# The last mixer half of a four-layer kernel in two passes of 256 tokens, and its late tiles' routing steps spaced differently

## The chip, the cores and the metric

The kernel runs on one core of one Trainium2 chip. The metric is the device time of one execution in microseconds (us). Engines are called as the profile calls them: PE is TensorE (PEld its weight loads), DVE is VectorE, ACT is ScalarE, POOL is GpSimd and SP the engine that issues most transfers.

## What is computed

2,048 tokens of 512 numbers pass through four residual layers, each behind a layer norm. The change touches the third layer and the routing of the fourth.

```python
x = x + scan_layer(norm(x))      # state space scan, 16 states
x = x + ffn_layer(norm(x))       # Hadamard transforms, gate / up / down
# third layer ("mixer"); y = conv(W_in_x . x) * D, z = silu(W_in_z . x)
x = x + einsum('bsi,hi->bsh', y * z, W_out)
# fourth layer: 64 experts, 8 per token, at most 128 tokens per expert
w, sel = top_k(softmax(x @ gate_w.T), 8)
pos = running_count_of_each_expert_over_tokens   # in token order
slot = where(pos < 128, pos, dropped)
out = down_e(silu(gate_e(inp)) * up_e(inp))      # per expert
x = x + weighted_sum_of_the_token's_experts
```

## The kernel before

Tokens are held in 4 chunks of 512, each of 4 tiles of 128 tokens, so there are 16 tiles. The ffn and mixer layers are cut into "halves" (list `HALVES`), and each half into **quanta**: for every 128 inner channels (a "pair") one gate quantum and one up quantum, and after them one down quantum per pair. A gate or up quantum is 12 products with 512 moving tokens (4 blocks of 128 inputs, times 3, since each operand is split into a high and a low part). Its weights are 512 KB, which come through a ring of 6 buffers: SP loads the buffer for quantum q + 6 as soon as quantum q has been used (`load_ring`).

Every engine runs a program that is written out by hand in **positions**. `spread` gives each position its quanta. At position p PE does the quantum of p, ACT and DVE work on the results of p - 1 and p - 2 (tanh, `half_gated`, `gated`, `gated_hi`, `gated_lo`), and everything else that an engine does in p stands behind that. In the stretch of this change every position has one quantum. The last mixer half (chunk 3, 8 pairs) starts at position TURN + 12; its down products are done after the loop by `tail(t, js)`, tile by tile.

**Routing** of a tile i has six steps, each in its own position, counted from `route_at[i]`. The steps, with their lines in the trace of before:

- `finished` (DVE, L1154 and L1407: mean and variance) and `rstd` (POOL, L1607 and L1609: reciprocal root, two instructions).
- `route(i, 0)` (DVE, L1368: the normalised tile `row`; it waits for `rstd(i)`).
- `route_T` (PE L568, then ACT L1080: transposes; they wait for `row`).
- `logits` (PE L784) and `route(i, 1)` (DVE, from L1372 to L1385, with `route_exp` on ACT).
- `place` (PE L790 and L791) and `route(i, 2)` (DVE, L1389 to L1396; the last writes `idx`).
- `rows_out` (POOL, L1600): eight indirect scatters of the tile's rows into the experts' slots, the first of which waits for `idx`.

Steps stand one position apart. Tiles 8 to 11 (chunk 2) start at TURN + 12 and every 4 positions after it; tiles 12 to 15 wait for the down products of the last half and are written out behind the loop. The position counter takes POOL through `rows_out(i)` in four positions with two scatters each, and `rstd` of a later tile stands where its position comes. SP starts the expert stage when all scatters have landed (L550, loads of `xe`).

Of the kernel before, what the change touches and what calls it, by code (L numbers as in the profile page):

```python
# [14 lines left out]
CH = 512  # L15
NCH = T // CH
# [22 lines left out]
MIX = [[("mixer", c, part, 4 * part, 4) for part in range(2)] for c in range(NCH - 1)] + [[("mixer", NCH - 1, 0, 0, M1)]]  # L39
# [12 lines left out]
H4 = hadamard(4).astype(int)  # L52


def build(nc, a):
# [47 lines left out]
    with top:  # L103
# [20 lines left out]
        with A:  # L124
# [176 lines left out]
            route_at = [DRAIN + 12 + 5 * i for i in range(EARLY)] + [TURN + 12 + 4 * i for i in range(TT)]  # L301
# [19 lines left out]
            def used(q):  # L321

                h, kind, j = quanta[q]
                if kind == "gate":
                    return S_g, first_pair[h] + j + 1
                if kind == "up":
                    return S_up, first_pair[h] + j + 1
                if j < pairs_of[h] - 1:
                    return S_dk, first_pair[h] - h + j + 1
                return S_dm, TT * (h + 1)  # L330
# [6 lines left out]
            def before_half(h):  # L337
# [4 lines left out]
                return half_of[kind, c, part - 1] if part else half_of["ffn", c, 1]  # L342

            with nc.Block() as block:
# [17 lines left out]
                def _(sp):  # L362
# [138 lines left out]
                    for pos in range(LAST):  # L501
# [23 lines left out]
                        if pos == TAIL + TT + 3:  # L525
                            sp.wait_ge(S_de, TT * len(HALVES))
# [12 lines left out]
                        if pos == TAIL - 6:  # L539
# [12 lines left out]
                    sp.wait_ge(S_dm, TT * len(HALVES))  # L552
# [11 lines left out]
                def _(pe):  # L564
# [11 lines left out]
                    def quantum(h, kind, j):  # L576
# [3 lines left out]
                        if kind != "down":  # L580
                            w = w.rearrange("p (k s c) -> p k s c", k=KT, s=2)
                            x = tokT[c % 2]
                            b = PF[2 * (j % 2) + (0 if kind == "gate" else 1)]
                            if kind == "gate":
# [12 lines left out]
                            for k in range(KT):  # L597
                                nc.tensor.matmul(b[:, :], w[:, k, 0, :], x[:, 0, k, :], start=(k == 0), stop=False)  # L598
                                nc.tensor.matmul(b[:, :], w[:, k, 0, :], x[:, 1, k, :], start=False, stop=False)  # L599
                                last = nc.tensor.matmul(b[:, :], w[:, k, 1, :], x[:, 0, k, :], start=False, stop=(k == KT - 1))  # L600
# [4 lines left out]
                        for t in range(TT):  # L605
# [12 lines left out]
                    def tail(t, js):  # L618
# [3 lines left out]
                        for j in js:  # L622
# [6 lines left out]
                            if (t, j) == (0, 0):  # L629
                                pe.wait_ge(S_de, TT * h)  # L630
# [166 lines left out]
                    for pos in range(DRAIN, TAIL):  # L797
# [10 lines left out]
                        for i, base in enumerate(route_at):  # L808
                            if pos == base + 4:
                                place(i)  # L810
                        for i, base in enumerate(route_at):
                            if pos == base + 3:
                                logits(i)
                        for i, base in enumerate(route_at):
                            if pos == base + 2:
                                route_T(i)
                        side(pos)
                    first_part, second_part = range(M1 // 2), range(M1 // 2, M1)
                    place(11)
                    tail(0, range(M1))  # L820
                    tail(1, first_part)
                    route_T(12)
                    tail(1, second_part)
                    logits(12)
                    tail(2, first_part)
                    place(12)
                    route_T(13)
                    tail(2, second_part)
                    logits(13)
                    tail(3, first_part)  # L830
                    place(13)
# [4 lines left out]
                    place(14)  # L836
# [871 lines left out]
```

## Time and profile before

| What | us |
|---|---|
| median of 3 runs | 1709.13 |
| lowest and highest of them | 1702.77, 1710.74 |
| the profiled execution | 1722.31 |
| its span, first to last instruction | 1720.5 |
| of the span: until the last mixer half starts | 1226 |
| from there to the last scatter | 119 |
| expert stage and sums after it | 375 |

The profiled execution is 1.8 us longer than its own span, and 13 us longer than the median. Instants below are microseconds from the start of the span.

### The profile page before, as it was taken

The page shows a single profiled execution, that of the slowest core. Times are in us where ns is not written, and L with a number is a line of the kernel's source. Part 1 is how long each engine was busy: PE and PEld are TensorE (multiplying, and loading weights), DVE is VectorE, ACT ScalarE, POOL GpSimd, SP SyncE. Part 2 cuts the span into 40 slices and gives each one's busy share as a digit, 9 for nine tenths or more (in the row PEclk, how much of TensorE's full clock was granted, in tenths as well). Part 3 has the DMA queues.
Part 4 walks back from the last instruction along what each step waited for, and adds up shares of the span by engine and source line. Part 5 has one row for each costly group of instructions (what it writes and reads, how often), then busy time and mean ns, then how long its engine had stood idle before and what let it go on. Part 6 is the DMA issues. An engine that isn't in the chain of part 4 may idle for free. (4 is left out here: it accounts for less than half of the span.)

```text
span 1720.5 us, 18848 instructions
## 1 busy us (share of the span) xinstructions
PE 1505.0 (87%) x5792; PEld 1038.6 (60%) x5792; DVE 1049.3 (61%) x1535; ACT 587.0 (34%) x1050; POOL 784.6 (46%) x483
## 2 busy tenths in 40 slices
PE   6989966899857999888999989999985699999990
PEld 2444323577645777776787878888874355555550
DVE  4887679798789887889888865452454122222220
ACT  4444633343534244534333332121321133233220
POOL 3467854253744345634445434773257322222232
PEclk8999987999978999999999999999997799999995
DMA  6899764256663666667565557998761599999997
GB/s 205 247 281 266 213 199 163 73 157 190 202 180 126 187 205 213 188 202 268 154 186 186 173 166 248 369 370 256 241 211 54 174 327 324 321 317 311 305 252 135
DMA packets 193539, 380.39 MB, mean 221 GB/s; under 512 B 20994, under 2 KB 95106, under 8 KB 192944
## 3 DMA queue, kind: packets, MB, share of 16 engines
q1 hardware_dynamic: 165360, 322.89, 59.7%
q0 software_dynamic: 20032, 39.92, 9.8%
q10 hardware_dynamic: 8064, 16.55, 2.8%
q8 instruction: 42, 0.69, 0.2%
q14 instruction: 41, 0.34, 0.1%
HBM read 301.65 MB, written 124.35 MB: 248 GB/s over the span
## 5 line engine op out<-in xcount | busy, mean ns | idle before, releaser
L1518 POOL TENSOR_TENSOR y<-y,hc 128x2048 f32<-128x2048 f32 x64 | 293.1, 4579 | 255.5 <-DVE hc L1350 255.5
L598 PE MATMUL bank<-tokT,ring 128*128 128x512 f32 x768 | 309.1, 402 | 13.9 <-DVE xall L1202 7.2
L1332 DVE TENSOR_TENSOR_SCAN bx<-bank,state,bx 128x512 f32<-128x512 f32 x256 | 312.7, 1267 | 0.8
L600 PE MATMUL bank<-tokT,ring 128*128 128x512 f32 x768 | 303.7, 395 | 0.0
L599 PE MATMUL bank<-tokT,ring 128*128 128x512 f32 x768 | 303.4, 395 | 0.0
L975 ACT ACTIVATE bank<-dl,an 128x512 f32<-128x512 f32 x256 | 171.0, 684 | 330.6 <-DVE bx L1332 330.5
L1524 POOL TENSOR_TENSOR act<-th,act 128x512 fp32r<-128x512 f32 x88 | 116.0, 1318 | 260.3 <-ACT act L899 259.7
L854 PE MATMUL bank<-wgu,xeT 128*128 128x384 f32 x512 | 178.5, 492 | 5.9 <-DMA wde<-wd_in 4.5
L598 PEld LDWEIGHTS bank<-tokT,ring 128*128 128x128 f32 x768 | 146.8, 191 | 50.6 <-issue 17.6
L600 PEld LDWEIGHTS bank<-tokT,ring 128*128 128x128 f32 x768 | 146.7, 191 | 32.4
L610 PE MATMUL bank<-ring,act 128*128 128x512 f32 x352 | 143.7, 408 | 24.7 <-DVE th L1182 19.4
L599 PEld LDWEIGHTS bank<-tokT,ring 128*128 128x128 f32 x768 | 146.8, 191 | 29.8
L1350 DVE TENSOR_TENSOR hc<-bx,bank 128x2048 f32<-128x2048 f32 x64 | 146.0, 2282 | 26.2 <-PE bank L686 25.6
L1323 DVE TENSOR_TENSOR bx<-u,bank 128x2048 f32<-128x2048 f32 x64 | 146.0, 2281 | 11.9 <-PE bank L678 8.8
L1600 POOL DMA_INDIRECT slots<-row,idx x128 | 127.0, 992 | 53.9 <-issue 41.4
L612 PE MATMUL bank<-ring,act 128*128 128x512 f32 x352 | 140.6, 399 | 0.0
L611 PE MATMUL bank<-ring,act 128*128 128x512 f32 x352 | 140.5, 399 | 0.0
L1175 DVE SCALAR_TENSOR_TENSOR th<-th,bank 128x512 f32<-128x512 f32 x96 | 65.7, 684 | 111.9 <-ACT th L894 96.7
L854 PEld LDWEIGHTS bank<-wgu,xeT 128*128 128x128 f32 x512 | 93.1, 192 | 60.4 <-issue 6.7
L1652 POOL DMA_INDIRECT acc<-ye,tok x32 | 49.3, 1541 | 163.6 <-DMA acc<-ye,tok 129.6
L871 PE MATMUL bank<-wde,hT 96*128 96x512 f32 x256 | 120.6, 593 | 0.5 <-DVE hT L1500 0.5
L1490 DVE SCALAR_TENSOR_TENSOR te<-te,bank 128x192 f32<-128x192 f32 x64 | 22.7, 354 | 154.0 <-ACT te L1123 154.0
(151 smaller groups left out, 2106.3 us busy)
## 6 DMA issues: line engine op xcount, KB each, us to landing
ring<-w_all SPq DMA_DIRECT2D x286, 512.0 KB
wgu<-wgu_in SPq DMA_DIRECT2D x64, 768.0 KB
wde<-wd_in SPq DMA_DIRECT2D x64, 384.0 KB
slots<-empty_in SPq DMA_DIRECT2D x16, 1154.0 KB, 8.8
w_all<-staged_u SPq DMA_DIRECT2D x64, 256.0 KB, 3.1
xe<-slots ACTq DMA_DIRECT2D x56, 288.5 KB
w_all<-fst SPq DMA_DIRECT2D x48, 256.0 KB, 3.8
w_all<-staged_d SPq DMA_DIRECT2D x32, 256.0 KB, 3.8
```

The lines of the kernel that those rows point to most:

```text
L598: nc.tensor.matmul(b[:, :], w[:, k, 0, :], x[:, 0, k, :], start=(k == 0), stop=False)
L599: nc.tensor.matmul(b[:, :], w[:, k, 0, :], x[:, 1, k, :], start=False, stop=False)
L600: last = nc.tensor.matmul(b[:, :], w[:, k, 1, :], x[:, 0, k, :], start=False, stop=(k == KT - 1))
L610: nc.tensor.matmul(PF[t][:, :], act8[:, 0, j, tok], w[:, 0, :], start=(j == 0), stop=False)
L611: nc.tensor.matmul(PF[t][:, :], act8[:, 0, j, tok], w[:, 1, :], start=False, stop=False)
L612: last = nc.tensor.matmul(PF[t][:, :], act8[:, 1, j, tok], w[:, 0, :], start=False, stop=(j == pairs - 1))
L854: last = nc.tensor.matmul(CG[i % 2][:, 0:2 * FE], xeT[:, i % 2, k, :], wgu[i][:, k, :], start=(k == 0), stop=(k == KT - 1))
L975: nc.scalar.activation(dA[k % 2][:, :], dl[c % 2][:, k, :], ACT.Exp, scale=an[:, k, n:n + 1]).then_inc(S_dA, 1)
L1323: nc.vector.tensor_tensor(bx[:, :, :], u[:, :, :], PB[:, :].unsqueeze(1).to_broadcast([P, KT, CH]), ALU.mult).then_inc(S_bm, 1)
L1332: nc.vector.tensor_tensor_scan(bx[:, k, :], dA[k % 2][:, :], bx[:, k, :], state[:, k, n:n + 1], ALU.mult, ALU.add).then_inc(S_sc, 1)
L1350: nc.vector.tensor_tensor(hc[:, :, :], bx[:, :, :], PC[:, :].unsqueeze(1).to_broadcast([P, KT, CH]), ALU.mult).then_inc(S_cm, 1)
L1518: nc.gpsimd.tensor_tensor(y[c % 2][:, :, :], y[c % 2][:, :, :], hc[:, :, :], ALU.add).then_inc(S_ya, 1)
```

## The change

The last mixer half becomes two (`LASTS`): the first takes tiles 12 and 13 (256 of the 512 tokens) through gate, up and down, the second tiles 14 and 15. Both use the same 8 pairs, so the weights of the gate and up quanta are loaded twice, and so are those of the down quanta but for the two that are held. Each gate or up quantum has 12 products of 256 moving tokens, each down quantum of the first pass 6 products (two tiles). Only the down products of tiles 14 and 15 are left to `tail`. The second pass swaps the PSUM banks (`pair_banks`), and its first gate waits for `gated` of the last pair before it.

Tiles 8 to 11 start every 6 positions in place of 4, tiles 12 and 13 get places in the loop (HALF1 and HALF1 + 4), and the steps of these six tiles stand 0, 1, 4, 6, 8 and 9 positions behind the tile's start in place of 0 to 5. Three loads of expert weights move to other positions of SP.

```diff
-MIX = [...] + [[("mixer", NCH - 1, 0, 0, M1)]]
+MIX = [...] + [[("mixer", NCH - 1, part, 0, M1) for part in range(2)]]
+LASTS = (len(HALVES) - 2, len(HALVES) - 1)
+def columns(h):
+    return slice(CH // 2 * LASTS.index(h), CH // 2 * LASTS.index(h) + CH // 2) if h in LASTS else slice(0, CH)
+def tiles_of(h):
+    return range(2 * LASTS.index(h), 2 * LASTS.index(h) + 2) if h in LASTS else range(TT)
+def pair_banks(h, j):
+    first = 2 * ((j + (h == LASTS[1])) % 2)
+    return first, first + 1
...
-            TAIL = TURN + 12 + 2 * M1
+            HALF1 = TURN + 12 + 3 * M1
+            TAIL = HALF1 + 2 * M1
-            spread([("mixer", 2, 1), ("mixer", 3, 0)], range(TURN, TAIL + RING))
+            spread([("mixer", 2, 1), ("mixer", 3, 0), ("mixer", 3, 1)], range(TURN, TAIL + RING))
-            route_at = [DRAIN + 12 + 5 * i for i in range(EARLY)] + [TURN + 12 + 4 * i for i in range(TT)]
+            route_at = [DRAIN + 12 + 5 * i for i in range(EARLY)] + [TURN + 12 + 6 * i for i in range(TT)] + [HALF1, HALF1 + 4]
+            ROUTE_EARLY, ROUTE_LATE = (0, 1, 2, 3, 4, 5), (0, 1, 4, 6, 8, 9)
+            route_step = [[base + d for d in (ROUTE_EARLY if i < EARLY else ROUTE_LATE)] for i, base in enumerate(route_at)]
...
-                        if pos == TAIL - 6:
+                        if pos == TURN + 26:
                             ...
                             load_weights(5, 5)
-                        if pos == TAIL - 1:
+                        if pos == HALF1 + 2:
                             ...
                             load_weights(6, 6)
-                        if pos == TAIL + 2:
+                        if pos == TAIL:
+                            sp.wait_ge(S_up, sum(pairs_of))
                             load_weights(7, 7)
...
                                 if j >= 2:
                                     pe.wait_ge(S_hg, i - 1)
+                                elif h == LASTS[1]:
+                                    pe.wait_ge(*((S_gt, i) if j == 0 else (S_de, adds_to(h) + 2)))
...
-                                nc.tensor.matmul(b[:, :], w[:, k, 0, :], x[:, 0, k, :], start=(k == 0), stop=False)
+                                nc.tensor.matmul(b[:, cols], w[:, k, 0, :], x[:, 0, k, cols], start=(k == 0), stop=False)
...
-                        for t in range(TT):
+                        for t in tiles_of(h):
...
-                    tail(0, range(M1))
-                    tail(1, first_part)
...
+                    tail(2, range(M1))
+                    tail(3, range(0, 3))
                     route_T(14)
-                    tail(3, second_part)
+                    tail(3, range(3, 5))
                     logits(14)
+                    tail(3, range(5, 7))
+                    place(14)
+                    tail(3, range(7, M1))
                     route_T(15)
...
-                            if pos == base + 4:
+                            if pos == at[4]:
                                 route(i, 2)
...
-                            if pos == base + 1:
+                            if pos == at[1]:
                                 route(i, 0)
```

The rows below are the engines' programs as built; a name with a number is a buffer, `bank4` to `bank7` hold the quanta's products, `n4_*` the statistics of routing.

On DVE, in the loop, the work that ends with `idx` of tile 9 and the work on `row` of tile 10, before:

```order
L1396 TENSOR_SCALAR idx<-top8 128x8 [waits route_step]
L1397 TENSOR_TENSOR chosen_sum<-chosen_sum,chosen_b 128x64
L1398 TENSOR_SCALAR number<-number 128x1
L1154 BN_STATS n4_st6<-xall 128x6 [waits down_added]
L1407 BN_AGGR n4_mvt<-n4_st6 128x2 [waits n4_bn]
L1175 SCALAR_TENSOR_TENSOR th<-th,bank4 128x512 [waits tanh_done]
L1191 TENSOR_TENSOR act8<-th,act8 128x512 [waits gated_hi,gated]
L1368 TENSOR_SCALAR row<-xall,n4_mvt,n4_rst 128x512 [waits n4_rs,rows_out2]
```

The same place in the changed program:

```order
L1174 BN_STATS n4_st6<-xall 128x6 [waits down_added]
L1430 BN_AGGR n4_mvt<-n4_st6 128x2 [waits n4_bn]
L1196 SCALAR_TENSOR_TENSOR th<-th,bank4 128x256 [waits tanh_done]
L1214 TENSOR_TENSOR act8<-th,act8 128x256 [waits gated_hi,gated]
L1391 TENSOR_SCALAR row<-xall,n4_mvt,n4_rst 128x512 [waits n4_rs,rows_out2]
L1204 SCALAR_TENSOR_TENSOR th<-bank5,cs,th 128x256 [waits half_gated,up_mm]
L1412 TENSOR_TENSOR rt<-bank3,rt 128x64 [waits place_mm]
L1413 TENSOR_SCALAR rt<-bank3 128x64
L1415 TENSOR_TENSOR rt<-rt 128x64 [waits route_step]
L1417 MAX top8<-rt 128x8 [waits route_step]
L1419 TENSOR_SCALAR idx<-top8 128x8 [waits route_step]
```

Before, `idx` of tile 9 was written ahead of the statistics of tile 10 and of its `row`. Now the statistics and `row` of tile 10 stand ahead of `idx` of tile 9.

On POOL, the last scatters (DMA `slots`) and `rstd` pairs (L1607, L1609) of before, from the last five scatters of tile 11 to the end of those of tile 13:

```order
L1600 DMA slots<-row,idx 8192x577 x5
L1607 TENSOR_TENSOR n4_vet<-n4_mvt,eps 128x1 [waits n4_mv,constants_ready]
L1609 TENSOR_TENSOR n4_rst<-n4_vet,neghalf 128x1 [waits n4_ve]
L1600 DMA slots<-row,idx 8192x577 [waits route_step]
L1600 DMA slots<-row,idx 8192x577
L1607 TENSOR_TENSOR n4_vet<-n4_mvt,eps 128x1 [waits n4_mv,constants_ready]
L1609 TENSOR_TENSOR n4_rst<-n4_vet,neghalf 128x1 [waits n4_ve]
L1600 DMA slots<-row,idx 8192x577 x6
L1607 TENSOR_TENSOR n4_vet<-n4_mvt,eps 128x1 [waits n4_mv,constants_ready]
L1609 TENSOR_TENSOR n4_rst<-n4_vet,neghalf 128x1 [waits n4_ve]
L1600 DMA slots<-row,idx 8192x577 [waits route_step]
L1600 DMA slots<-row,idx 8192x577 x7
```

And of the change, from the last seven scatters of tile 12 to the end of those of tile 15:

```order
L1614 DMA slots<-row,idx 8192x577 x7
L1614 DMA slots<-row,idx 8192x577 [waits route_step]
L1614 DMA slots<-row,idx 8192x577 x7
L1621 TENSOR_TENSOR n4_vet<-n4_mvt,eps 128x1 [waits n4_mv,constants_ready]
L1623 TENSOR_TENSOR n4_rst<-n4_vet,neghalf 128x1 [waits n4_ve]
L1614 DMA slots<-row,idx 8192x577 [waits route_step]
L1614 DMA slots<-row,idx 8192x577 x2
L1621 TENSOR_TENSOR n4_vet<-n4_mvt,eps 128x1 [waits n4_mv,constants_ready]
L1623 TENSOR_TENSOR n4_rst<-n4_vet,neghalf 128x1 [waits n4_ve]
L1614 DMA slots<-row,idx 8192x577 x5
L1614 DMA slots<-row,idx 8192x577 [waits route_step]
L1614 DMA slots<-row,idx 8192x577 x7
```

Before, the `rstd` of tiles 14 and 15 stood ahead of most of the scatters of tiles 12 and 13. Now the `rstd` of tile 14 stands behind all the scatters of tiles 12 and 13. In both programs the loop has each `rstd(i + 2)` behind all eight scatters of tile i, for i of 8 to 10.

## Rows read from the trace of the kernel before

**Rows 1.** Busy time by stage; the header names the columns, (x) counts instructions.

```profile
core 0: us, PE busy (x) PEld busy (x) DVE busy (x) ACT busy (x) POOL busy (x), PEclk, DMA share, GB/s
1226.00:1311.00 85.00, 78.65 (x382) 63.37 (x381) 43.88 (x154) 17.63 (x41) 42.97 (x52) 0.98 0.60 195
1311.00:1346.00 35.00, 4.07 (x22) 3.39 (x21) 7.27 (x38) 1.78 (x7) 26.42 (x29) 0.54 0.11 31
1346.00:1720.50 374.50, 323.46 (x1152) 186.62 (x1152) 81.88 (x320) 96.55 (x192) 102.07 (x68) 0.94 0.99 283
```

**Rows 2.** The chain that ended last, where the expert stage begins: start us, us, what.

```profile
1346.51 2.95 DMA xe<-slots
1349.50 1.97 PE bank L845 x8
```

**Rows 3.** Costliest group of the stretch 1226 to 1346.

```profile
L1600 POOL DMA_INDIRECT slots<-row,idx x64 | 63.2, 988 | 25.6 <-issue 23.1 <-DVE idx L1396 2.6
```

**Rows 4.** GpSimd in order of time: start us, us, instruction [idle before <-releaser].

```profile
1242.71 1.04 POOL L1600 DMA_INDIRECT slots<-row,idx  x1 [0.19 <-issue]
...
1257.55 1.04 POOL L1600 DMA_INDIRECT slots<-row,idx  x1 [0.19 <-issue]
...
1266.55 0.97 POOL L1600 DMA_INDIRECT slots<-row,idx  x1 [0.31 <-issue]
...
1291.23 0.23 POOL L1607 TENSOR_TENSOR n_vet<-n_mvt,eps 128x1 f32<-128x1 f32 x1
1291.54 0.57 POOL L1609 TENSOR_TENSOR n_rst<-n_vet,neghalf 128x1 f32<-128x1 f32 x1
...
1301.93 1.04 POOL L1600 DMA_INDIRECT slots<-row,idx  x1 [2.57 <-DVE idx L1396]
...
1306.40 1.04 POOL L1600 DMA_INDIRECT slots<-row,idx  x1 [0.19 <-issue]
...
1344.34 0.97 POOL L1600 DMA_INDIRECT slots<-row,idx  x1 [0.30 <-issue]
```

**Rows 5.** VectorE in order of time, same columns.

```profile
1240.41 0.17 DVE L1396 TENSOR_SCALAR idx<-top 128x8 uint32<-128x8 f32 x1
...
1269.65 0.21 DVE L1389 TENSOR_TENSOR rt<-bank,rt 128x64 f32<-128x64 f32 x1
...
1270.55 0.17 DVE L1396 TENSOR_SCALAR idx<-top 128x8 uint32<-128x8 f32 x1
...
1292.21 0.55 DVE L1368 TENSOR_SCALAR row<-xall,n_mvt,n_rst 128x512 f32<-128x512 f32 x1 [1.48 <-POOL n_rst L1609]
...
1300.95 0.17 DVE L1396 TENSOR_SCALAR idx<-top 128x8 uint32<-128x8 f32 x1
...
1314.80 0.55 DVE L1368 TENSOR_SCALAR row<-xall,n_mvt,n_rst 128x512 f32<-128x512 f32 x1 [0.80 <-POOL n_rst L1609]
...
1321.89 0.42 DVE L1396 TENSOR_SCALAR idx<-top 128x8 uint32<-128x8 f32 x1
```

**Rows 6.** The page's groups of instructions: two widths of one VectorE operation.

```profile
L1175 DVE SCALAR_TENSOR_TENSOR th<-th,bank 128x512 f32<-128x512 f32 x96 | 65.7, 684 | 111.9 <-ACT th L894 96.7
...
L1490 DVE SCALAR_TENSOR_TENSOR te<-te,bank 128x192 f32<-128x192 f32 x64 | 22.7, 354 | 154.0 <-ACT te L1123 154.0
```

**Rows 7.** TensorE in order of time.

```profile
1261.38 1.00 PE L784 MATMUL bank<-gate,x4T 128*128 128x64 f32 x8
1262.18 0.48 PE L598 MATMUL bank<-tokT,ring 128*128 128x512 f32 x1
...
1267.94 0.39 PE L598 MATMUL bank<-tokT,ring 128*128 128x512 f32 x1
...
1270.43 0.39 PE L600 MATMUL bank<-tokT,ring 128*128 128x512 f32 x1
```

**Rows 8.** A window in which transfers fill the DMA engines, columns as in the first group.

```profile
1241.00:1248.00 7.00, 7.00 (x36) 5.64 (x35) 3.03 (x6) 1.98 (x4) 4.81 (x7) 1.00 1.03 351
```

**Rows 9.** DMA issues between 1226 and 1346.

```profile
ring<-w_all SPq DMA_DIRECT2D x17, 512.0 KB
```

More of the change, by code:

```diff
@@ L38 @@
 FFN = [[("ffn", c, part, HALF * part, HALF) for part in range(2)] for c in range(NCH)]
-MIX = [[("mixer", c, part, 4 * part, 4) for part in range(2)] for c in range(NCH - 1)] + [[("mixer", NCH - 1, 0, 0, M1)]]
+MIX = [[("mixer", c, part, 4 * part, 4) for part in range(2)] for c in range(NCH - 1)] + [[("mixer", NCH - 1, part, 0, M1) for part in range(2)]]
 HALVES = FFN[0] + [h for c in range(2, NCH + 1) for h in MIX[c - 2][:1] + FFN[c - 1] + MIX[c - 2][1:]] + MIX[NCH - 1]
@@ L341, in before_half @@
                     return None
-                return half_of[kind, c, part - 1] if part else half_of["ffn", c, 1]
+                return half_of[kind, c, part - 1] if part and h not in LASTS else half_of["ffn", c, 1]
             with nc.Block() as block:
@@ L582, in quantum @@
                             x = tokT[c % 2]
-                            b = PF[2 * (j % 2) + (0 if kind == "gate" else 1)]
+                            cols = columns(h)
+                            b = PF[pair_banks(h, j)[0 if kind == "gate" else 1]]
                             if kind == "gate":
@@ L807, in _ @@
                                 mixer_T(c, t)
[L808 to L809 removed]
+                        for i, at in enumerate(route_step):
+                            if pos == at[4]:
                                 place(i)
[L811 to L812 removed]
+                        for i, at in enumerate(route_step):
+                            if pos == at[3]:
                                 logits(i)
[L814 to L815 removed]
+                        for i, at in enumerate(route_step):
+                            if pos == at[2]:
                                 route_T(i)
                         side(pos)
[L818 to L831 removed]
+                    tail(2, range(M1))
+                    tail(3, range(0, 3))
                     route_T(14)
[L833 removed]
+                    tail(3, range(3, 5))
                     logits(14)
+                    tail(3, range(5, 7))
+                    place(14)
+                    tail(3, range(7, M1))
                     route_T(15)
[L836 removed]
                     logits(15)
@@ L893, in tanh @@
                         wait(act, S_al, i - 1)
-                        nc.scalar.activation(th[:, i % 2, :], PF[2 * (j % 2)][:, :], ACT.Tanh, scale=gsh[:, m:m + 1]).then_inc(S_th, 1)
+                        cols = columns(h)
+                        nc.scalar.activation(th[:, i % 2, cols], PF[pair_banks(h, j)[0]][:, cols], ACT.Tanh, scale=gsh[:, m:m + 1]).then_inc(S_th, 1)
                     def gated_hi(h, j):
@@ L898, in gated_hi @@
                         i = first_pair[h] + j
-                        nc.scalar.activation(act8[:, 0, j, :], th[:, i % 2, :], ACT.Copy).then_inc(S_ah, 1)
+                        cols = columns(h)
+                        nc.scalar.activation(act8[:, 0, j, cols], th[:, i % 2, cols], ACT.Copy).then_inc(S_ah, 1)
                     def prep_hi(i, m):
@@ L1108, in _ @@
                     side(TAIL + 1)
-                    for i in range(3 * TT, NCH * TT):
+                    for i in range(len(route_at), NCH * TT):
                         route_T(i)
@@ L1528, in side @@
                         for h, kind, j in quanta_at.get(pos - 2, ()):
-                            if kind == "up" and h < len(HALVES) - 1:
+                            if kind == "up" and h not in LASTS:
                                 gated_lo(h, j)
```

102 lines of the change are left out of this document (46 added, 56 removed).

## Prediction

> **What bounds the kernel now.** I read the stages first. From 1226, where the last mixer half starts, PE is busy for 78.7 of 85 us, but from 1311 to 1346 for only 4.1 of 35, while POOL is busy for 26.4 of those 35 and DMA is idle at a share of 0.11 [rows 1]. The chain of waits enters the expert stage through the `xe` loads at 1346.51 and PE follows at 1349.50 [rows 2]; the loads wait for the last scatter. So the stretch ends with POOL, not with PE. There are 64 scatters in it, of 988 ns each [rows 3]; eight of them take 9.97 us from the first one's start (1257.55) to the last one's end (1267.52) [rows 4], so one is 1.28 us with its gap. From 1306.40 to the end at 1345.31 POOL does nothing but scatter, apart from one `rstd` [rows 4]. Whatever PE gains is worth something only if POOL's last scatter ends sooner. The expert stage behind it (374.5 us [rows 1]) is untouched.
>
> POOL has 64 times 1.28 = 82 us of scatters and started at 1242.71 [rows 4], so 21 of the 103 us until 1345.31 are waits and `rstd`. That is what the change can win or lose.
>
> **PE and DMA with 256 tokens.** Twelve 512-token products from the start of 1267.94 to that of 1270.43 are 11 steps, 226 ns each [rows 7], so a quantum is 2.72 us. 512 columns at 2.4 GHz are 213 ns, so 13 are fixed. For 256 columns no row exists. From below, half of 226: 113. From above, a weight load that could not hide: eight loads with 64 columns each pass in 0.80 us (1261.38 to 1262.18 [rows 7]), 100 ns per pair, and 107 ns of streaming behind it gives 207. I take 107 + 13 = 120 ns, since the 100 ns row shows that loads can come at that rate: a quantum is 1.45 us. All quanta of the half then cost 32 x 1.45 + 8 x 1.36 (first pass down) + 24 x 2 x 0.226 (tail) = 68.1 us against 16 x 2.72 + 96 x 0.226 = 65.2 before: 3 us more on PE.
>
> By the Trainium skill, TensorE: Matmul & The Clock Gate, section Back-to-back issue gap, a warm product takes N/2.4 + 2.5 ns. At 512 columns this case's row has 226 where the rule has 216; at 256 the rule would give 109 ns in place of 120 and start the first scatter about 1 us sooner.
>
> Ring loads: 46 quanta have weights of 512 KB [rows 9], 40 of them loaded after the half starts, 21 MB. The x store, the two held blocks and three experts' weights that fall into the stretch add about 5.6 MB by the sizes in the program. When full, DMA moves 351 GB/s (share 1.03) [rows 8]: 76 us. PE needs 68 plus eight tiles of routing at 1.3 (0.4 transposes, 0.8 logits [rows 7], 0.1 place), 78 us. So DMA is nearly as full as PE; ring waits of up to 4 us are likely near the held and expert loads, but PE has slack against POOL, as follows.
>
> **The order of POOL and DVE.** This is the term that decides. Scatters of tile i, then `rstd(i + 2)` is POOL's order before and now. Before, `idx(i + 1)` stood on DVE ahead of `row(i + 2)`; now it stands behind it, and `row(i + 2)` waits for `rstd(i + 2)`. So tile i + 1 cannot start scattering until all eight scatters of tile i are done, then `rstd`, `row`, a `gated`, the five instructions of `route(i + 1, 2)`, and the wake of POOL. One turn:
>
> - eight scatters, 9.97 [rows 4];
> - `rstd`, 0.88 (1291.23 to 1292.11) [rows 4];
> - to the start of `row` 0.10, `row` 0.55 [rows 5];
> - `gated` on 256 columns: 684 ns at 512 columns, 354 at 192 [rows 6], so 0.42 on that line; the second operation is a little slower, and I take 0.48, which stands in two of the three turns (a down position has none);
> - `route(., 2)` from 1269.65 to 1270.72, 1.07 [rows 5];
> - `idx` written (1301.12 [rows 5]) to scatter (1301.93 [rows 4]), 0.81;
> - less 0.2 for neighbouring records on DVE that overlap.
>
> That is 13.7 (13.2 without `gated`), of which POOL idles 2.8. PE's own pace over six positions is 6 x 1.45 + 1.3 = 10.0 us, so POOL and DVE set the pace and PE waits 3 to 4 us per tile. ACT and DVE queues behind `row` (tanh results, `gated`) are late with it, and PE's `route_T` of that tile too, but all of that waits for the same `rstd`. These waits also hide the ring's.
>
> The Trainium skill says, in TensorE: Matmul & The Clock Gate, section Architectural detail: the array is 16× 32×32, not 1× 128×128, that ScalarE, VectorE and GpSimd run their queues strictly first in, first out; only weight loads overtake. The trace agrees: DVE's `row` at 1292.21 waited for `n_rst` and everything on DVE with it [rows 5].
>
> **The sum.** `idx(8)` ended at 1240.58 [rows 5]. Now eight short quanta stand ahead of it in place of four long ones (11.6 for 10.9, +0.7), and `finished(9)` and `row(9)` are now ahead of it on DVE (+0.8): 1242.1. POOL wakes 0.81 later: scatters of tile 8 at 1242.9 (before 1242.71, since `rstd(9)` was in the way).
>
> - Tiles 9, 10, 11 start at 1256.6, 1269.8, 1283.5 (turns of 13.7, 13.2, 13.7).
> - Tile 11's scatters have `rstd(13)` in their middle (+0.8), so they end at 1294.3; `idx(12)` comes about then, four more position's work on DVE after `row(13)`: tile 12 at 1295.
> - Tile 12 and 13 run on, 10.2 each: done at 1315.2. PE's tail for tile 14 ends near 1309 and waits.
> - `rstd(14)` 1316.1, `row(14)` 1316.2. Tile 15's chain from `row` to `idx` took 7.5 before (1314.80 to 1322.31 [rows 5]), at the low clock (0.54 granted [rows 1]). Tile 14's now has 12 products of tile 15 between its steps, 2.7 us at 0.226, of which most hide behind ACT and DVE steps: 8.3. `idx(14)` 1324.5, three scatters from 1325.3 to 1328.9.
> - `rstd(15)`, `row(15)` at 1329.9; `idx(15)` 7.5 later, 1337.4; the five remaining scatters of tile 14 are done by 1336.3. Wake 0.81, eight scatters 9.97: **1348.2**.
>
> Before, 1345.31 [rows 4]: +2.9 us. The profiled 1722.3 would become 1725.2; on the median of the runs, 1709.1 + 2.9 = **1712**. The x store of the last chunk leaves at about 1327 and takes some 5 us, still under the scatters. The moved expert loads are wanted from 1350 on and are covered.
>
> **Rivals.**
>
> - *The order costs nothing and POOL packs.* Were each `idx` ready when POOL is, 1242.9 + 82 + six `rstd` of 0.8 = 1330, a gain of 15 us: 1694. For it speaks that tiles 12 and 13 are routed in the loop, and that PE is ahead of POOL. Against it is the built order of DVE. If only the loop's three idles (2.8, 2.3, 2.8) vanished, the end would be 1340, 1704, which is within 0.5%. It ends under 1700.6 if 8.5 us of POOL's 19 idle go. Chance 0.13.
> - *Weight loads set the pace of 256 columns.* At 190 ns per product (the upper half of the bounds) a quantum is 2.3 us and six positions with routing 15 us, more than the turn of 13.7. `idx(8)` is 5.5 us later, the two turns whose six positions are gate and up quanta are 1.3 longer, and two more positions' groups for tile 12: about +9 to +12 on the sum, 1721 to 1724. From about 165 ns on this decides. Against it: the 100 ns row. Chance 0.15.
> - *DMA cannot feed the ring.* At 300 GB/s, 27 MB are 89 us, 11 more than PE needs; PE's tail would end near 1318, just past tile 13's last scatter, and everything behind shifts by some 3 to 8: 1715 to 1720. 351 in the row speaks against it. Chance 0.10, half of it slower by over 0.5%.
> - *The turn is as computed* (POOL, then DVE): 0.62, end between 1343 and 1353, 1707 to 1717.
>
> **How the numbers follow.** A measurement of this kernel can tell 0.5% from no change, 8.5 us: 1700.6 to 1717.7. Faster 0.13, same 0.62 from the forecast and 0.05 from DMA, slower 0.15 and 0.05. The range takes in the packed case's nearer part and the weight load case: 1700 to 1724.
>
> **What the profile would show.** Right: `rstd` of tiles 10 to 12 on POOL directly behind the eighth scatter, `row` on DVE with a wait for `n_rst`, scatters of tiles 9 to 11 starting 13 to 14 us apart with POOL idle for 2 to 3 us ahead of each; products of 256 columns 120 ns apart; POOL idle for about 9 us between tiles 13 and 14; last scatter ending 105 us after tile 8's first. Wrong: products 160 ns apart or more; PE waits named `ring` of over 5 us in all; `idx` waits gone from POOL.

## Result, and the profile after

The changed kernel took 1726.29 us (median of 20 runs, 1714.49 to 1737.76), the kernel before 1711.07 us (20 runs, 1702.77 to 1721.57): a ratio of 1.0091, 95% interval 1.0071 to 1.0111. It is 15 us slower. The forecast was 1712, with a range from 1700 to 1724, so the measured time lies outside it.

The profiled execution of the changed kernel took 1714.62 us, below its median, as that of the kernel before took 1722.31, above its own. So whole spans of the two profiles can't be compared. I compare stretches, from a landmark that the change doesn't touch: the last `gated_lo` with 512 columns on POOL, the last piece of the half ahead of the change. POOL in order of time, changed kernel (start us, us, instruction, idle before and its releaser):

```profile
1208.96 1.29 POOL L1538 TENSOR_TENSOR act<-th,act 128x512 fp32r<-128x512 f32 x1 [4.30 <-ACT act L919]
...
1236.48 1.04 POOL L1614 DMA_INDIRECT slots<-row,idx  x1 [2.84 <-DVE idx L1419]
...
1252.21 0.19 POOL L1621 TENSOR_TENSOR n_vet<-n_mvt,eps 128x1 f32<-128x1 f32 x1 [5.74 <-DVE n_mvt L1430]
...
1255.97 1.04 POOL L1614 DMA_INDIRECT slots<-row,idx  x1 [2.85 <-DVE idx L1419]
...
1269.30 1.04 POOL L1614 DMA_INDIRECT slots<-row,idx  x1 [2.45 <-DVE idx L1419]
...
1283.86 1.04 POOL L1614 DMA_INDIRECT slots<-row,idx  x1 [3.69 <-issue]
...
1325.25 1.04 POOL L1614 DMA_INDIRECT slots<-row,idx  x1 [8.75 <-DVE idx L1419]
...
1347.61 0.97 POOL L1614 DMA_INDIRECT slots<-row,idx  x1 [0.30 <-issue]
```

The scatters at 1236.48, 1255.97, 1269.30 and 1283.86 are the first ones of tiles 8 to 11, and 1325.25 is the first of tile 14. The prediction had POOL idle for 2 to 3 us ahead of tiles 9, 10 and 11 and for about 9 us ahead of tile 14; the rows have 2.85, 2.45, 3.69 and 8.75. One wait it didn't have: at 1252.21 POOL waits 5.74 us for the mean and variance of tile 10. Tile 8 starts 27.5 us behind the landmark, tile 9 only 19.5 us later, and the last scatter starts 138.7 us behind the landmark. The kernel before has its landmark, in the same view, here:

```profile
1215.25 1.29 POOL L1524 TENSOR_TENSOR act<-th,act 128x512 fp32r<-128x512 f32 x1 [4.29 <-ACT act L899]
```

and the last scatter at 1344.34 [rows 4], 129.1 behind it. The stages of the changed kernel, to be held against [rows 1]:

```profile
core 0: us, PE busy (x) PEld busy (x) DVE busy (x) ACT busy (x) POOL busy (x), PEclk, DMA share, GB/s
1226.00:1311.00 85.00, 70.95 (x489) 65.69 (x487) 40.51 (x163) 18.64 (x53) 47.39 (x55) 0.92 0.95 322
1311.00:1348.60 37.60, 13.22 (x56) 10.13 (x55) 9.34 (x42) 2.38 (x8) 20.97 (x24) 0.69 0.18 51
```

In the first row, DMA went from a share of 0.60 to 0.95, while PE is busy for 8 us less: it waits. PE in order of time shows where:

```profile
1241.44 0.58 PE L626 MATMUL bank<-tokT,ring 128*128 128x256 f32 x1 [6.86 <-DMA ring<-w_all]
```

This wait has a second price. Windows of 4 us show the granted clock, first right behind the wait, then 4 us later:

```profile
1240.00:1244.00 4.00, 2.56 (x12) 2.56 (x12) 0.00 (x0) 0.00 (x0) 3.00 (x4) 0.50 1.04 391
...
1248.00:1252.00 4.00, 4.00 (x36) 4.00 (x36) 3.30 (x16) 1.38 (x5) 0.00 (x0) 1.00 0.99 363
```

PE had been idle for 6.86 us, and the clock is then at 0.50 (1.2 GHz): the first quantum behind the wait takes 2.73 us (1241.44 to 1244.17), where the forecast for one at full clock was 1.45.

DVE, changed kernel: `row` of tile 11 and `idx` of tile 10 stand in the order that was read from the program, `row` with its wait for `rstd`:

```profile
1266.95 0.55 DVE L1391 TENSOR_SCALAR row<-xall,n_mvt,n_rst 128x512 f32<-128x512 f32 x1 [4.91 <-POOL n_rst L1623]
...
1268.32 0.17 DVE L1419 TENSOR_SCALAR idx<-top 128x8 uint32<-128x8 f32 x1
```

### The profile page after: what moved, and what is told of

It reads as the page before. It is cut to its first block and busy times, and to the rows that moved or that the text cites. A ratio compares the mean times of both kernels' runs of the same rounds, so it can differ in the third digit from the quotient of the medians.

```text
span 1712.8 us, 19327 instructions
## 1 busy us (share of the span) xinstructions
PE 1505.7 (88%) x5984; PEld 1052.3 (61%) x5984; DVE 1052.1 (61%) x1559; ACT 590.0 (34%) x1066; POOL 785.5 (46%) x483
## 5 line engine op out<-in xcount | busy, mean ns | idle before, releaser
L626 PE MATMUL bank<-tokT,ring 128*128 128x512 f32 (+1 forms) x832 | 321.2, 386 | 20.2 <-DMA ring<-w_all 10.0
L628 PE MATMUL bank<-tokT,ring 128*128 128x512 f32 (+1 forms) x832 | 315.4, 379 | 0.0
L627 PE MATMUL bank<-tokT,ring 128*128 128x512 f32 (+1 forms) x832 | 315.2, 379 | 0.0
L626 PEld LDWEIGHTS bank<-tokT,ring 128*128 128x128 f32 x832 | 160.0, 192 | 54.7 <-issue 17.2
L628 PEld LDWEIGHTS bank<-tokT,ring 128*128 128x128 f32 x832 | 160.0, 192 | 29.6
L627 PEld LDWEIGHTS bank<-tokT,ring 128*128 128x128 f32 x832 | 160.2, 193 | 27.5
L638 PE MATMUL bank<-ring,act 128*128 128x512 f32 x368 | 152.0, 413 | 23.9 <-DVE th L1204 16.6
L639 PE MATMUL bank<-ring,act 128*128 128x512 f32 x368 | 147.3, 400 | 0.0
L640 PE MATMUL bank<-ring,act 128*128 128x512 f32 x368 | 147.1, 400 | 0.0
L1196 DVE SCALAR_TENSOR_TENSOR th<-th,bank 128x512 f32<-128x512 f32 (+1 forms) x104 | 66.7, 641 | 105.5 <-ACT th L913 105.4
## 6 DMA issues: line engine op xcount, KB each, us to landing
wgu<-wgu_in SPq DMA_DIRECT2D x64, 768.0 KB, 15.2
wde<-wd_in SPq DMA_DIRECT2D x64, 384.0 KB, 13.7
```

What stands on the lines that cost most here:

```text
L626: nc.tensor.matmul(b[:, cols], w[:, k, 0, :], x[:, 0, k, cols], start=(k == 0), stop=False)
L627: nc.tensor.matmul(b[:, cols], w[:, k, 0, :], x[:, 1, k, cols], start=False, stop=False)
L628: last = nc.tensor.matmul(b[:, cols], w[:, k, 1, :], x[:, 0, k, cols], start=False, stop=(k == KT - 1))
L638: nc.tensor.matmul(PF[t][:, :], act8[:, 0, j, tok], w[:, 0, :], start=(j == 0), stop=False)
L639: nc.tensor.matmul(PF[t][:, :], act8[:, 0, j, tok], w[:, 1, :], start=False, stop=False)
L640: last = nc.tensor.matmul(PF[t][:, :], act8[:, 1, j, tok], w[:, 0, :], start=False, stop=(j == pairs - 1))
```

## Experiments

All are timed beside the kernel before on the same chip. I state the two theories that I started from. First: the spacing of the steps (`ROUTE_LATE`) costs it, by the turn. Second: transfers cost it, since the second pass loads 12 MB again. The first expectations call them Theory A and Theory B; later ones give the letters anew. Every run's stretch stands in one table at the end of this section.

**The changed kernel again.** No edit.

> The changed kernel, unaltered, profiled and timed once more beside the kernel before. In its first profile the stretch from the first rstd of tile 8 to the last scatter took 125.7 us against 116.1 before, 9.6 us more, while the medians differ by 15 us. If all of the loss lies in this stretch, the stretch varies from execution to execution and this profile shows one near 131 us. If about 5 us are lost elsewhere, the stretch is again near 126 us and the expert stage or the stages ahead of it are longer than before.

1725.62 us (10 runs), ratio 1.0086 (1.0060 to 1.0112). The stretch repeats within 0.3 us (138.4 after 138.7), so the first case of the expectation, a longer stretch this time, is out. The second case, 5 us lost outside it, is taken up with the short kernels. This profiled execution too is short, 1710.12 us and 15.5 below its own median, with the same stretch: what made it short lies outside the stretch.

**The old spacing of the steps.**

```diff
-            ROUTE_EARLY, ROUTE_LATE = (0, 1, 2, 3, 4, 5), (0, 1, 4, 6, 8, 9)
+            ROUTE_EARLY, ROUTE_LATE = (0, 1, 2, 3, 4, 5), (0, 1, 2, 3, 4, 5)
...
-                    rows_out(13, 6)
-                    rows_out(13, 7)
```

> The change with one part undone: the late tiles keep their starts but have their routing steps 0 to 5 positions behind them again, so idx of tile i + 1 stands ahead of row of tile i + 2 on VectorE. Theory A (the order of POOL and DVE sets the pace): the turns from tile 9 to 10 and 10 to 11 fall from 13.3 and 14.6 us to about 11.1, and the kernel gains 4 to 6 us on the change. Theory B (ring loads set the pace): the first turn stays near 19 us with a ring wait near 7 us, and the later ones stay over 13 us too, since the engines now wait for weights, so the kernel gains under 2 us. The two can both be partly right; the turns tell them apart one by one.

1724.71 us (7 runs), 1.0094 (1.0057 to 1.0131): no gain, and neither expectation came true. Tile 8 starts 6 us sooner, but the turns (from the first scatter of one tile to that of the next) are 15 to 16 us. PE's wait of 6.86 us for the ring is down to 0.3, though no load was moved: PE waits for `row` instead. POOL of this kernel shows why, in order of time:

```profile
1229.23 1.06 POOL L1614 DMA_INDIRECT slots<-row,idx  x1 [7.93 <-DVE idx L1419]
...
1233.14 0.98 POOL L1614 DMA_INDIRECT slots<-row,idx  x1 [0.30 <-issue]
1234.12 0.22 POOL L1621 TENSOR_TENSOR n_vet<-n_mvt,eps 128x1 f32<-128x1 f32 x1
...
1244.92 0.97 POOL L1614 DMA_INDIRECT slots<-row,idx  x1 [4.89 <-DVE idx L1419]
```

and DVE:

```profile
1235.09 0.55 DVE L1391 TENSOR_SCALAR row<-xall,n_mvt,n_rst 128x512 f32<-128x512 f32 x1 [2.76 <-POOL n_rst L1623]
...
1243.96 0.17 DVE L1419 TENSOR_SCALAR idx<-top 128x8 uint32<-128x8 f32 x1
```

`rstd(9)` now stands behind four scatters of tile 8, and 8.9 us pass from `row(9)` to `idx(9)`. Four scatters (4.9), `rstd` and the step to `row` (1.0), `row` to `idx` (8.9) and POOL's wake (1.0) are the 15.7 us. With tiles six positions apart this spacing only puts the wait elsewhere, so this run doesn't test the turn of the prediction.

**Expert loads behind the last half's weights.** The changed kernel issues the held blocks and expert 4 at TURN + 14, amid the ring's loads, and experts 5 and 6 later, at TURN + 26 and HALF1 + 2.

```diff
-                        if pos == TURN + 14:
+                        if pos == TURN + 30:
...
+                        if pos == TAIL:
...
                             load_weights(4, 4)
-                        if pos == TURN + 26:
...
                             load_weights(5, 5)
-                        if pos == HALF1 + 2:
...
                             load_weights(6, 6)
-                        if pos == TAIL:
```

(Of the first block only the held blocks are left at TURN + 30; experts 4, 5 and 6 go to TAIL.)

> The change with 3.5 MB of expert weights (experts 4, 5 and 6) loaded behind the last ring load in place of among them, and the two held blocks loaded 16 positions later; the routing steps stay as in the change. Theory B (the first turn of 19.5 us is a wait for the ring behind the held blocks and expert 4): the wait of 6.9 us on PE goes, the first turn falls to 13.7 us, and the stretch and the time fall by 5 to 7 us. Theory A alone: the turn is bound by the scatters and rstd anyway and the gain is under 2 us.

1720.50 us (12 runs), 1.0061 (1.0035 to 1.0086). PE's wait of 6.86 us for the ring is gone (1.2 us in all are left in the stretch), tile 9's turn falls from 19.5 to 13.7, and the stretch from 138.7 to 131.3. One window of both, the changed kernel first:

```profile
1226.00:1241.00 15.00, 8.58 (x74) 8.33 (x72) 7.28 (x29) 3.54 (x10) 4.42 (x6) 0.96 1.03 357
```

```profile
1226.00:1241.00 15.00, 15.00 (x129) 14.96 (x129) 9.21 (x34) 5.43 (x15) 2.10 (x4) 1.00 0.97 363
```

DMA moves the same 357 and 363 GB/s in both; what differs is whose bytes they are. PE is busy for 8.58 us in one and for all 15 in the other. SP of the changed kernel, in order of time:

```profile
1225.10 1.52 SPq L561 DMA_DIRECT2D held<-w_all  x2
1226.66 0.46 SPq L520 DMA_DIRECT2D wgu<-wgu_in  x1
1227.17 0.48 SPq L523 DMA_DIRECT2D wde<-wd_in  x1
1227.69 17.03 SPq L453 DMA_DIRECT2D ring<-w_all  x7
```

Two held blocks of 512 KB, 768 KB and 384 KB are 2.2 MB, 6.2 us at 357 GB/s, and PE waited for 6.86. The kernel before issues the same four at the same position, with quanta of 2.72 us around them, and its PE waited for the ring for 1.2 us in the first profile and not at all in the second.

**Both.**

> Both edits together: steps 0 to 5 and the expert weights behind the ring loads. If A and B each hold a part, nothing but POOL's scatters is left between tiles 8 and 13: turns of about 11.1 us, tile 13's last scatter at 66 to 70 us from tile 8's first, and the stretch falls from 125.7 to 108 to 114 us, so 12 to 17 us faster than the change and 2 to 8 us faster than before. If PE with 256-token products is slower than I take it, the turns stay above 12 us with DVE waiting for PE.

1727.99 us (6 runs), 1.0097 (1.0060 to 1.0134). The edits of the two kernels above together. Forecast were turns of 11.1 us and 12 to 17 us less than the change; the turns stay at 14 to 17 us and nothing is gained. With the old spacing the ring isn't what ends the waits: between 1226 and 1300 PE waits 15.1 us for `row`, and DVE's `row` 14.7 us for `rstd`.

One question was then open: the stretch with the loads behind was 131.3 us against 129.1 in the profile of before, 2.2 us, and the medians stood 11.5 us apart. So I cut off most of the stage behind the stretch, and profiled the kernel before once more.

**Short kernels and the kernel before again.** 24 of the 64 experts in every engine:

```diff
+ER = 24
...
-                    for e in range(E):
+                    for e in range(ER):
```

(and `E // DEEP` as `ER // DEEP` where the experts' loops end.)

> The kernel before with 24 of the 64 experts (the 40 others are left out in every engine, so most of the MoE sum is missing; all stages ahead of the experts are whole). It is the base for the two other short kernels. The full kernels' profiles put the stretch from the last 512-column gated product on POOL to the last scatter at 129.0 us before, 138.7 us in the changed kernel and 131.2 us with the expert loads behind, while their medians stand 15 and 11.5 us above the kernel before. Theory A (all that the change costs is in that stretch): the medians of the short kernels stand apart as the full ones do, and full profiles of the same median would show it. Theory B (part of the cost falls in the expert stage, whose transfers are busy all the time): the short kernels stand apart by the stretch alone, since two thirds of the expert stage are gone. Expected of this one: 40 experts at 5.6 to 5.8 us less than the kernel before, 1479 to 1487 us.

> The changed kernel with 24 of the 64 experts (40 left out). Theory A: 15 us over the short kernel before. Theory B: 9.6 us over it (the stretch alone) and up to a third of the other 5 us. Theory C (the cost lies ahead of the last half): also 15 us, but the last 512-column gated product on POOL would stand later than in the short kernel before by some 5 us.

> The changed kernel with the expert loads 4 to 6 behind the last half's weights, with 24 of the 64 experts (40 left out). Theory A: 11.5 us over the short kernel before. Theory B: 2.2 us over it and up to a third of the other 9 us, so 2 to 5 us.

> The kernel before, unchanged. A ratio of 1.000 within 0.002, and a second profile. The first had the last 512-column gated product on POOL at 1215.3 us, the last scatter 129.0 us later and 376 us from there to the end, at a time 11 us above the median. If the expert stage is what scatters, this one shows 362 to 370 us there at a time near 1709 us; if the stages ahead scatter, the landmark stands 5 to 8 us earlier.

Short before 1492.84 us (5 runs, 1492.19 to 1497.36), short change 1512.57 (5 runs, 1506.92 to 1515.18), short with the loads behind 1502.91 (5 runs, 1499.55 to 1503.30). The base was expected at 1479 to 1487 and missed that: 40 experts took 218 us, 5.5 each. The two others stand 19.7 and 10.1 us above it, so the missing time does not lie in the expert stage, and Theory B of these three falls. Theory A (15 and 11.5) is nearer, but asks for a shorter stretch in the kernel before than the first profile has. Nor is it ahead of the landmark, as Theory C had it: that stood at 1209.5 in the short kernel before, and at 1211.4 and 1205.2 in the two others. The kernel before again: 1709.74 us (12 runs), ratio 0.9995 (0.9971 to 1.0019). Its profile was expected to be shorter in the expert stage or ahead of the landmark. The landmark did come 9.6 us sooner, while the part behind the last scatter was 5 us longer; the stretch is what answers the question, POOL in order of time:

```profile
1205.61 1.29 POOL L1524 TENSOR_TENSOR act<-th,act 128x512 fp32r<-128x512 f32 x1 [4.30 <-ACT act L899]
...
1233.05 1.04 POOL L1600 DMA_INDIRECT slots<-row,idx  x1 [0.19 <-issue]
...
1245.68 1.04 POOL L1600 DMA_INDIRECT slots<-row,idx  x1 [0.19 <-issue]
...
1258.27 1.04 POOL L1600 DMA_INDIRECT slots<-row,idx  x1 [0.19 <-issue]
...
1327.51 0.97 POOL L1600 DMA_INDIRECT slots<-row,idx  x1 [0.30 <-issue]
```

Tiles 8 to 10 start 12.6 us apart, not 14.8 and 15.3, and the last scatter starts 121.9 us behind the landmark, not 129.1. The short kernel before has the same turns and 121.8. So the execution whose profile stands ahead of the prediction was the odd one. These two profiles come from one chip, but the medians on the other chips fit them as well: a stretch of 126.2 us (below) goes with a median 4.5 us above the kernel before, which is its distance from 121.9, not from 129.1. DVE's waits in the first profile between 1226 and 1311 (engine, what waited, for what: us in total, times, longest):

```profile
DVE th L1175 <- ACT th L894: 9.3, 4, 3.3
DVE th L1175 <- issue: 8.7, 2, 5.0
DVE th L1182 <- remote: 8.4, 3, 3.8
DVE xall L1202 <- PE bank L634: 6.7, 3, 2.3
DVE xall L1202 <- issue: 3.6, 1, 3.6
```

and in the same window of the kernel before again (the three longest):

```profile
DVE th L1175 <- ACT th L894: 15.8, 7, 3.3
DVE xall L1202 <- PE bank L634: 11.1, 4, 3.6
DVE row L1368 <- POOL n_rst L1609: 1.9, 2, 1.1
```

Six waits for which the trace names no instruction of another engine, 20.7 us in all, are in the first only; part of each may be a wait that would have been there for ACT or PE. Five more of them, of 1.6 to 5.2 us, stand ahead of the stretch, between 1076 and 1163. The first and the second that fall before an `idx`:

```profile
1253.61 0.75 DVE L1182 SCALAR_TENSOR_TENSOR th<-bank,cs,th 128x512 f32<-128x512 f32 x1 [2.17 <-remote]
...
1268.98 0.75 DVE L1182 SCALAR_TENSOR_TENSOR th<-bank,cs,th 128x512 f32<-128x512 f32 x1 [3.82 <-remote]
```

In the kernel before again, `gated` (L1182) started right behind the steps of `route(i, 1)` at this place, without idle time.

**The indices ahead of the row.** If the turn is what the prediction says, putting `idx(i + 1)` ahead of `row(i + 2)` again, with tiles still six positions apart, must shorten it. On top of the loads behind:

```diff
-            ROUTE_EARLY, ROUTE_LATE = (0, 1, 2, 3, 4, 5), (0, 1, 4, 6, 8, 9)
+            ROUTE_EARLY, ROUTE_LATE = (0, 1, 2, 3, 4, 5), (0, 1, 3, 5, 6, 7)
...
-                    rows_out(13, 6)
-                    rows_out(13, 7)
```

> As with the expert loads behind, and the late tiles' steps at 0, 1, 3, 5, 6, 7 in place of 0, 1, 4, 6, 8, 9, so that on DVE the indices of tile i + 1 stand ahead of the row of tile i + 2, as in the kernel before. With the loads behind, the last scatter stood 131.2 us behind the last 512-column gated product on POOL (before: 121.9), and the turns of tiles 9 to 12 took 13.7, 13.3, 14.6 and 11.6 us. Theory A (the turn: POOL waits for the indices, which wait for the row, which waits for rstd behind eight scatters): tile 8 starts 2 to 3 us sooner, the turns fall to 11 to 12 us, PE waits less for the rows and ends its tail up to 8 us sooner, and the last scatter stands 123 to 126 us behind the landmark: 1712 to 1716. Theory B (256 columns on PE and the ring's 12 MB more set the pace): the waits turn into waits of PE for the ring, and the end moves by under 3 us: 1718 to 1722.

1714.13 us (12 runs), 1.0021 (0.9999 to 1.0042); the stretch is 126.2 us, the turns 11.2, 11.2 and 11.9. Theory A holds. The edit also brings the steps of a tile closer together, by which tile 8 starts 2.2 us sooner; of the 9.5 us gained up to tile 11, 4.5 are lost again at tiles 12 to 14. Then `rstd(15)` behind the first scatter of tile 14 in place of the third:

```diff
-                    for k in range(3):
-                        rows_out(14, k)
+                    rows_out(14, 0)
                     rstd(15)
-                    for k in range(3, TOPK):
+                    for k in range(1, TOPK):
```

> As e4_idx_ahead, and on POOL the rstd of tile 15 stands behind the first scatter of tile 14 in place of the third. With the loads behind, n_mvt of tile 15 was ready at 1321.7 and its rstd ran at 1324.5 to 1325.3, and the scatters of tile 14 ended 3.6 us before tile 15's indices. The row, and with it the last eight scatters, come 2.2 us sooner than in e4_idx_ahead, if tile 15's chain sets the end; no change, if the scatters of tile 14 do. Against the kernel before: same or up to 0.3% slower.

> As e5_idx_ahead_rstd with 24 of the 64 experts (the 40 others are left out, so most of the MoE sum is missing). The short kernel before has a median of 1492.8, the short changed one 1512.6, the short one with the loads behind 1502.9. Theory A: 1492 to 1497. Theory B: 1499 to 1502.

1710.85 us (12 runs), 1.0009 (0.9989 to 1.0028), and short 1495.57 (6 runs, 1491.30 to 1502.07). The last turn falls from 13.4 to 11.2, as expected. POOL of the full one, in order of time:

```profile
1236.46 0.63 POOL L1620 TENSOR_TENSOR n_rst<-n_vet,neghalf 128x1 f32<-128x1 f32 x1
1237.27 1.04 POOL L1611 DMA_INDIRECT slots<-row,idx  x1 [0.17 <-issue]
...
1247.38 0.21 POOL L1618 TENSOR_TENSOR n_vet<-n_mvt,eps 128x1 f32<-128x1 f32 x1
...
1248.43 1.04 POOL L1611 DMA_INDIRECT slots<-row,idx  x1 [0.19 <-issue]
...
1258.55 0.21 POOL L1618 TENSOR_TENSOR n_vet<-n_mvt,eps 128x1 f32<-128x1 f32 x1
...
1259.59 1.04 POOL L1611 DMA_INDIRECT slots<-row,idx  x1 [0.19 <-issue]
...
1316.20 1.04 POOL L1611 DMA_INDIRECT slots<-row,idx  x1 [7.17 <-DVE idx L1416]
```

From tile 8 to tile 10 POOL goes from tile to tile without a wait for DVE. What is left are 1.02 us ahead of tile 11, 2.85 ahead of tile 12 and the 7.17 us ahead of tile 14. At last the steps alone, without the moved loads:

> The changed kernel with the late tiles' steps at 0, 1, 3, 5, 6, 7 alone; the expert loads stay where the change has them. Known so far, from the last 512-column gated product on POOL to the last scatter: before 121.9 us, change 138.7, loads behind 131.2, both edits 126.2. If the two faults lie one behind the other on the way to the end (first the ring starves PE, then the turns are long), the edit is worth 5 us here as well: 133 to 134 us, 1720 to 1722 by the clock of the runs. If the ring's shortage takes all that the shorter turns give back, since PE would then only wait longer for the ring: 137 to 139 us, 1724 to 1727.

1723.59 us (12 runs), 1.0080 (1.0049 to 1.0111). The stretch is 135.4 us: between the two expectations. PE still waits 5.8 us for the ring, tile 9's turn is 18.8 us, the turns behind it are 11.2 and 12.3; of the 5.1 us that the steps gave with the loads behind, 3.3 are left.

Stretches in us, from one profile each: landmark to first scatter of tile 8, turns to tiles 9 to 15, landmark to the start of the last scatter, and how far the median stands from that of the kernel before in the same comparison (for the short kernels, from that of the short kernel before; the last of them was timed on another chip than it).

```
                       tile 8   turns to tiles 9 .. 13       14    15    last   median
before, first profile    27.5   14.8 15.3 14.8 14.2 13.0   10.3  10.2   129.1
before, again            27.4   12.6 12.6 12.1 14.7 13.0   10.3  10.2   121.9
short before             27.4   12.6 12.6 12.1 14.7 12.9   10.2  10.2   121.8
change                   27.5   19.5 13.3 14.6 11.6 10.2   19.5  13.4   138.7   +15.2
change again             27.6   18.6 13.3 14.6 11.6 10.3   20.2  13.4   138.4   +16.7
old spacing              21.7   15.7 15.1 16.1 16.3 10.5   23.4  13.4   141.2   +15.7
loads behind             27.5   13.7 13.3 14.6 11.6 10.2   18.0  13.4   131.3   +11.5
both                     21.8   16.0 15.0 13.7 17.0 10.5   23.5  13.3   139.8   +19.0
idx ahead, loads behind  25.3   11.2 11.2 11.9 13.8 10.7   19.8  13.4   126.2    +4.5
the same, rstd sooner    25.3   11.2 11.2 11.9 13.8 10.3   20.6  11.2   124.4    +1.2
idx ahead alone          25.3   18.8 11.2 12.3 13.8 10.4   21.1  13.4   135.4   +11.2
short change             27.5   19.2 13.3 14.5 11.6 10.3   19.5  13.4   138.3   +19.7
short loads behind       27.5   13.7 13.3 14.5 11.6 10.2   17.9  13.4   131.1   +10.1
short, rstd sooner       25.3   11.1 11.2 11.9 13.9 10.3   20.5  11.2   124.4    +2.7
```

Against 121.9, the stretches are longer by 16.8, 19.3, 9.4, 17.9, 4.3, 2.5 and 13.5 us (change, old spacing, loads behind, both, and the three full kernels with `idx` ahead); the medians follow within 4 us.

## Why the prediction was wrong

**The base: wrong, and the largest error.** The step that failed is "Before, 1345.31 [rows 4]: +2.9 us" on a median of 1709.1. The sum was made against a profile in which DVE's unnamed waits had lengthened three turns by 2.2, 2.7 and 2.7 us; the two other profiles of the same code up to there have 7.2 us less between landmark and last scatter. The median does not hold those 7.2 us, so adding +2.9 to it mixed two executions. The profile said so: its time was 13.2 us over the median, its rows gave tile starts 14.8 us apart, and its own PE rows give four quanta at 2.72 and 1.3 of routing, 12.2 us, for the same four positions. The prediction had both numbers and did not ask who took the rest. Without this error the same working gives +10.1 us, 1719, "slower".

**The ring: mechanism seen as a rival, size wrong.** The step that failed is "DMA is nearly as full as PE; ring waits of up to 4 us are likely near the held and expert loads, but PE has slack against POOL". It compared sums over the whole half, 76 and 78 us. The rate counts: a quantum of 512 KB every 1.45 us is 362 GB/s, and a full DMA moved 351 [rows 8] and here 357. So little else fits between gate and up loads, and the 2.2 MB of held blocks and expert 4, issued there, became one wait of 6.86 us. The slack was not there either: tile 8's scatters had only begun at 1236.48, and tile 10's `finished`, which waits behind the starved products, was late by 5.74 us for POOL. Cost: 5.8 us in tile 9's turn, shown by moving the loads. The sum had no term for PE's clock either, which was at 0.50 behind the wait. PE's waits named `ring` add up to 10.0 us, where the prediction had put over 5 us down as a sign of being wrong. Its rival priced a shortage at 3 to 8 us, but from a rate of 300 GB/s over the whole half; the rate was as high as in the row, and the loads came too close together.

**The turn: right.** 13.7, 13.2, 13.7 us were forecast; with the loads behind it is 13.7, 13.3, 14.6, and in the changed kernel the two turns that the ring doesn't disturb are the same 13.3 and 14.6. Undoing the order of `idx` and `row` took them to 11.2, 11.2 and 11.9, with no wait of POOL for `idx` at tiles 9 and 10, and 1.02 us of idle time ahead of tile 11. PE's waits for `row` were 2.0 and 2.2 us with the loads behind, not 3 to 4. DVE sat idle for 4.91 us ahead of `row` at 1266.95, and `idx` at 1268.32 behind it, though PE's last product for `idx` (L819) had started at 1262.22. The rule of the Trainium skill that was cited there (TensorE: Matmul & The Clock Gate, section Architectural detail: the array is 16× 32×32, not 1× 128×128, on strictly ordered queues) agrees with these two rows. The 0.9 us by which the third turn is over the forecast lie on POOL: from `idx` of tile 11, written at 1282.20, to its first scatter at 1283.86 it is 1.66 us, where the sum took 0.81 from tile 12. The kernel before has 1.65 at tile 11 (1286.05 to 1287.70); why is open. But the turn was judged against 14.8; against the usual 12.6, 12.6 and 12.1 it is a loss of 0.7 to 2.5 us each, where the sum counted a gain.

**256 columns: right.** Products start 0.12 us apart (nine steps from 1220.13 to 1221.19 are 1.06 us, 118 ns each; the forecast was 120); PE:

```profile
1220.13 0.28 PE L627 MATMUL bank<-tokT,ring 128*128 128x256 f32 x1
...
1221.19 0.28 PE L627 MATMUL bank<-tokT,ring 128*128 128x256 f32 x1
```

So the rival with weight loads as the bound falls. (Its sum was also off: eight quanta at 2.28 us in place of 1.45 are 6.6 us, not 5.5.) The rule of the Trainium skill (TensorE: Matmul & The Clock Gate, section Back-to-back issue gap), stated there for an isolated product, makes it 109 ns, 9 less than the row.

**Tiles 14 and 15: right.** The prediction put tile 14 20.1 us behind tile 13, the trace has 19.5; the last eight scatters 12.9 us later, the trace has 13.4. The kernel before has 10.3 and 10.2 there. These two are the price of the two passes: tile 14 can't be routed before the whole second pass is through. They cost 12.4 us, of which 5.9 come back at tiles 12 and 13.

The terms add up: +2.9 forecast, +7.2 base, +5.8 ring, +0.9 third turn, are 16.8 us; the stretch is longer by 16.8 (other steps differ from the forecast by 0.6 us at most and cancel), and the runs by 15.2 and 16.7. POOL's last scatter was forecast to end at 1348.2 and ended at 1348.6, which is chance: everything up to the landmark ran 6.3 us sooner in that execution.

What stays open: what held DVE in the first profile (no run provoked it), and 3 us of the 19.7 by which the short change stands above the short kernel before (its stretch is longer by 16.5).

## What to carry to other kernels

Before a time of one execution becomes the base, ask whether that execution is like the others: where it stands against the runs' median, and whether an engine on the path has waits that no instruction explains. Where a phase gets faster, compute the rate it then asks of DMA, bytes of one step by the time of one step, and not the sum over the stage; whatever else is issued in that phase is paid for: here 2.2 MB became a wait of 6.86 us, with PE at half clock behind it. In engines that run in order, an instruction that waits for a late engine goes behind all that the late engine itself needs next (POOL was late for DVE's `row`, and needed DVE's `idx` next): writing the indices two positions sooner, ahead of the row that waited, was worth 5 us here.

## What was not expected of the hardware

The loop over the experts is the same code in all full kernels, but the stretch between the last scatter and the end took 363.0 to 381.3 us, while with 24 experts it took 161.1 to 162.3. The kernel before again has the longest, 381.3, in an execution of 1710.7 us. DMA is full in this stage, and moves more in some executions than in others. One window of the changed kernel and the same of the kernel before again:

```profile
1550.00:1600.00 50.00, 50.00 (x182) 29.11 (x181) 12.70 (x50) 15.06 (x30) 14.13 (x10) 1.00 1.05 321
```

```profile
1550.00:1600.00 50.00, 46.10 (x162) 25.82 (x161) 11.54 (x43) 13.56 (x27) 12.32 (x8) 1.00 1.05 306
```

At the same share of 1.05, it is 321 and 306 GB/s, and with the lower rate PE runs short. And DVE had six waits of 2 to 5 us without a named releaser within 45 us in one execution of the kernel before, and none in the two others that were profiled; what held it is not known.
